# First two tiles of the second layer's attention projected two steps earlier, in a two-layer transformer block

## The reference

```python
def _layer(x, wqkv, qs, ksc, wo, lg, lb, w1, b1, w2, b2):
    h = shift_token(x)                       # second half of the features from the token before
    q, k, v = split(h @ wqkv)                # 8 heads of 64
    q, k = l2norm(q) * qs, l2norm(k) * ksc
    q, k = rotary_xpos(q, k)
    x = x + local_attention(q, k, v) @ wo
    h = shift_token(x)
    mu, var = h.mean(-1), h.var(-1)
    h = (h - mu) / sqrt(var + 1e-05) * lg + lb
    a, g = split(h @ w1 + b1)
    return x + (a * gelu(g)) @ w2 + b2

for l in range(2):                           # DEPTH
    x = _layer(x, wqkv[l], ...)
```

## Time and profile before

| | us |
|---|---|
| median of 3 runs | 1131.87 (1130.56 to 1132.34) |
| profiled execution, its own time | 1133.57 |
| profiled execution, span from first to last instruction | 1131.8 |
| TensorE busy in the span | 1062.1 |
| GpSimd busy in the span | 747.3 |
| VectorE busy in the span | 833.3 |
| ScalarE busy in the span | 670.9 |

### The profile page before, as it was taken

One profiled execution on the slowest core, in us unless ns is written; L12 is line 12 of the kernel. 1 busy time (PEld: TensorE's weight loads), 2 busy tenths in 40 slices (PEclk: granted clock), 3 DMA queues, 4 the chain that ended last, 5 costly groups with the idle time before them and its releaser, 6 DMA issues. The chain is left out here.

```text
span 1131.8 us, 23099 instructions
## 1 busy us (share of the span) xinstructions
PE 1062.1 (94%) x8304; PEld 654.9 (58%) x8304; DVE 833.3 (74%) x1522; ACT 670.9 (59%) x1222; POOL 747.3 (66%) x510
## 2 busy tenths in 40 slices
PE   6884799999999999999999999889999797999988
PEld 3552455555555555555555554766677694776778
DVE  6995666666666666666666674589999689999857
ACT  2552366566665665666666655047887556887744
POOL 3662466767686767776676768679986238756526
PEclk9996799999999999999999999999999999999989
DMA  8899622524315124242152100101111100111101
GB/s 255 276 275 357 161 57 48 112 53 93 80 50 122 40 66 104 67 92 69 48 113 71 44 20 21 38 10 32 33 43 34 25 2 19 33 34 33 44 17 36
DMA packets 82624, 88.48 MB, mean 78 GB/s; under 512 B 32036, under 2 KB 65360, under 8 KB 82512
## 3 DMA queue, kind: packets, MB, share of 16 engines
q1 hardware_dynamic: 82512, 87.01, 29.9%
HBM read 53.04 MB, written 24.24 MB: 68 GB/s over the span
## 5 line engine op out<-in xcount | busy, mean ns | idle before, releaser
L871 DVE CUSTOM_DVE_ANT_0 junk<-psum,alibi 128x1024 bf16<-128x1024 f32 x256 | 313.2, 1223 | 200.7 <-PE psum L942 191.8
L843 ACT ACTIVATE E<-psum,keybias_sb 128x1024 f32<-128x1024 f32 x256 | 274.7, 1112 | 229.6 <-PE psum L966 216.3
L774 POOL TENSOR_TENSOR sum_p<-sum_p,E 128x1024 f32<-128x1024 f32 x96 | 232.4, 2421 | 90.4 <-ACT E L843 85.8
L978 PE MATMUL psum<-E,V 128*64 128x512 f32 x1024 | 248.1, 605 | 0.0
L942 PE MATMUL psum<-KH,QH 64*128 64x512 f32 x512 | 118.7, 459 | 12.9 <-PEq L274 7.4
L978 PEld LDWEIGHTS psum<-E,V 128*64 128x64 f32 x1024 | 62.2, 136 | 112.3 <-issue 98.4
L780 POOL TENSOR_TENSOR sum_p<-sum_p,xpos_sb 128x1024 f32<-128x1024 f32 x32 | 76.3, 2384 | 69.0 <-DVE xpos_sb L881 69.0
L942 PEld LDWEIGHTS psum<-KH,QH 64*128 64x128 f32 x512 | 49.5, 189 | 121.9 <-DVE M L871 84.5
L966 PE MATMUL psum<-QH,KH 64*128 64x512 f32 x512 | 102.2, 395 | 2.1 <-DVE M L871 2.1
L966 PE MATMUL psum<-QL,KH 64*128 64x512 f32 x512 | 101.6, 392 | 0.0
L966 PE MATMUL psum<-QH,KL 64*128 64x512 f32 x512 | 101.5, 392 | 0.0
(11 more groups left out here) (149 smaller groups left out, 2008.3 us busy)
## 6 DMA issues: line engine op xcount, KB each, us to landing
QH<-qa_scratch SPq DMA_DIRECT2D x64, 256.0 KB, 4.2
qa_scratch<-tH SPq DMA_DIRECT2D x8, 1024.0 KB, 5.4
qa_scratch<-tL SPq DMA_DIRECT2D x8, 1024.0 KB, 7.9
QL<-qa_scratch SPq DMA_DIRECT2D x64, 128.0 KB, 4.2
vp_att<-v_att SPq DMA_DIRECT2D x64, 128.0 KB, 2.3
XF<-inverse_scratch SPq DMA_DIRECT2D x30, 256.0 KB, 3.4
KH<-k_scratch SPq DMA_DIRECT2D x16, 256.0 KB, 3.9
KL<-k_scratch SPq DMA_DIRECT2D x16, 256.0 KB, 5.1
```

What stands on the lines that cost most here:

```text
L774: pool.tensor_tensor(sum_p[:, s, :], first, E[:, k % 4, :], ALU.add)\
L843: act.activation(E[:, k % 4, :], scores(k % 2), ACT.Exp, bias=kb).then_inc(exp_done, 1)
L871: dve.tensor_tensor_reduce(junk[:, :], banks(max_bank(i, k), 2), alibi[:, s, :], -1.0, BIG, ALU.add, ALU.min, M[:, s, k:k + 1]).then_inc(m ...
L978: last = pe.matmul(banks(6 + i % 2)[HD * ch:HD * ch + HD, :], V[:, g, k, :], E[:, k % 4, ch * 512:(ch + 1) * 512], start=(k == 0), stop=(k ...
```

## The change

The stages of attention 1 with lags 0, 1 and 2 (TURN_X, PROJECT and NORMS, on all engines) run two steps earlier for tiles 0 and 1. They now stand in steps 31 to 34, where the MLP of layer 0 still works on its last tiles; for the other 14 tiles they keep their steps, and all stages with a lag of 3 and more are as before. Within a step the order of the stages is the same: each stage's early half stands where the stage stood.

```diff
-        parts = []
+        parts, second_attention = [], []
+        EARLY_TILES, EARLY_STEPS, EARLY_LAGS = 2, 2, 3
@@
+            if l > 0:
+                second_attention.append(attention)
             parts += [(attention, LAYER_STEPS * l)] + (output if l == 0 else []) + [(mlp, LAYER_STEPS * l + MLP_STEP)]
 
+        def early(fn, lag):
+
+            def some_tiles(t, s):
+                if t < EARLY_TILES:
+                    fn(t, s)
+
+            return some_tiles, lag - EARLY_STEPS
+
+        def other(fn, lag):
+
+            def some_tiles(t, s):
+                if t >= EARLY_TILES:
+                    fn(t, s)
+
+            return some_tiles, lag
+
         def stages(engine, handle):
 
-            return [(fn, lag + first) for part, first in parts if engine in part for fn, lag in part[engine](handle)]
+            found = []
+            for part, first in parts:
+                for fn, lag in part[engine](handle) if engine in part else ():
+                    if first >= LAYER_STEPS and lag < EARLY_LAGS and part in second_attention:
+                        found += [early(fn, lag + first), other(fn, lag + first)]
+                    else:
+                        found.append((fn, lag + first))
+            return found
```

## The result

The changed kernel took 1136.85 us (median of 11 runs, 1134.04 to 1138.42), the kernel before 1132.01 us beside it. The ratio is 1.0038, with a 95% interval of 1.0026 to 1.0051: slower by some 4.3 us, and by more than the 0.2% that can be told from no change. The forecast was 1135.3 us, +3.4, with a range of 1131.0 to 1137.0; inside it, the case of the forecast itself was given +2.8 to +4.2. The span went from 1131.8 to 1135.0 us. The lines of this kernel.py are 26 higher than before from the second half on (L1485 is the old L1459).

What follows compares the result with a forecast made beforehand. Latency where the two layers meet was taken to bound the kernel, not throughput. Terms 0.2 + 1.5 + 0.9 + 1.3 - 0.5 gave +3.4 us, median 1131.87 to 1135.3 us; range 1131.0 to 1137.0.

Steps and rivals of the forecast that it cites:

- the case of the forecast itself: Between the two layers, two delays of ln_apply by GpSimd's rotation plus a low TensorE clock: +2.8 to +4.2 us, chance 0.4.
- the seam: Stretch between the two layers, said to be latency-bound; measured from MLP tile 10's XF write to layer 1 tile 2's mask product.
- the power rival: GpSimd's power on tile 1 also blocks VectorE's normalise of tile 0 in layer 1: +4.5 us, 1136.4 us, chance 0.12.
- Term 1: Layer 1's first tiles: two long TensorE waits come back as three shorter ones, behind MLP turn, square and gate: +0.2 us.
- the ring: Pace-setting loop from project_qk through rotary products and square to the next project_qk; 5.25 us, 6.7 through ln_apply.
- Term 2: ln_apply of MLP tile 14 waits on VectorE for GpSimd's rotation additions of tile 0, delaying the second project_qk: +1.5 us.
- Term 3: TensorE falls to 1.2 GHz on layer 1's second project_qk, 3.20 instead of 1.88 us: +0.9 us.
- Term 4: ln_apply of MLP tile 15 waits on VectorE for GpSimd's two rotation additions of tile 1: +1.3 us.
- Term 5: VectorE's normalise of tile 1 in layer 1 takes some 1.4 instead of 1.96 us, with less GpSimd addition left: -0.5 us.
- The power: GpSimd's power of tile 1 overlaps VectorE's normalise of tile 0; no wait was taken, with a bound of +1.1 us.
- The faster rival: TensorE's 1.25 and 2.09 us waits between the layers really go: -3.3 us, or -4.6 without the low clock; chance 0.08.

## Why the prediction was right

The mechanism was right, and the seam's +3.58 us is close to the sum of +3.4. The whole time fits less well than that: the median of 1136.85 us lies only 0.15 below the top of the range, and the +4.3 us of the ratio is just outside the +2.8 to +4.2 of the forecast's own case and nearer to the +4.5 of the power rival. Only the rows tell these two apart. That the median still fell inside the range is partly luck.

By its own steps; positions in the changed trace are lowered by 0.46 us, by which TensorE's rows ahead of the seam lie later than in the earlier trace rows.

- *Term 1, the ring without collisions, +0.2.* With rotation and ln_apply parted, the first mask product came 20.23 us after the XF write of tile 10 (946.65 and 926.42) against 20.12 before: +0.1. The ring of 6.7 us is 6.65. Right in size; it came back as four waits, not three, and the +0.1 is taken against a kernel with a low clock.
- *Term 2, first collision, +1.5.* ln_apply ended at 931.70, forecast 931.8. Right, and the choice between its bounds too: the second addition goes ahead of ln_apply's second instruction in both traces.
- *Term 3, the clock, +0.9.* project_qk took 3.45 and 3.60 us; its last product ended at 938.36, forecast 938.2. The filled gaps, at 1.39 us, priced it together with what it does to the second collision.
- *Term 4, second collision, +1.3.* ln_apply of tile 15 ended at 941.03, forecast 940.8. Right in size, for a partly different reason: the rotation of tile 1 was released by the late products (0.42 us idle, DVE t_att, before 938.97), not by the end of the power.
- *Term 5, normalise of tile 1, -0.5.* 1.36 us instead of 1.96: -0.6.
- *Sum.* The first mask product stands at 949.45, forecast 949.2, and the seam is +3.58 (second traces: +3.71) where the sum said +3.4. By the experiments it is -0.47 without the collisions, where terms 1 and 5 said -0.3, and +4.05 for collisions and clock, where terms 2 to 4 said +3.7. The median's +4.3 has the seam's value in its interval. Its excess of 0.7 us over the seam is less than the part behind the last mask product varies from one execution to the next.
- *The power.* normalise of tile 0 ran from 946.80 to 948.02 with GpSimd's power from 944.98 to 947.91 around its start and took 1.22 us. It waited for nothing, as the prediction had it, in every trace of a kernel with the two tiles early (1.21 or 1.22 us). The prediction had argued from an ln_apply row, which has one tile as its input and not two, so that row alone could not decide it. The rule of the Trainium skill (SBUF — State Buffer, "Who interferes with whom"), by which the two exclude each other for the whole instruction, agrees with the rows of GpSimd's additions (normalise at 939.85) and not with that of its power. The rival with +4.5 us falls by this row.
- *The faster rival* named its own point of decision, VectorE at ln_apply before the rotation starts. It came 0.6 us after it (930.20 and 929.64). Even without the collisions the seam gained only 0.47 us, not 3.3, and that was the low clock: the waits came back behind ln_apply, turn and hT copy. With ln_apply out of the ring 1.9 us of them were gained (33.37 against 35.26 us), which shows that it was in the way; 1.51, 0.67 and 0.76 us of waits were still left on TensorE.

## What to carry to other kernels

Moving a stage ahead in an in-order schedule moves it behind other neighbours on every engine: write down, for each engine, what stands between a producer and its consumer in the new order before counting on an idle gap. When two stages that take turns between engines are interleaved, look first at the place of the one whose result feeds the longest chain. Here ln_apply of two tiles, four instructions of 128x64, moved by one step took 6.4 us from the changed kernel's seam (39.97 to 33.52), while the change itself had added 3.6; the whole time shows some 4 us of it (a ratio to the kernel before of 0.9999 instead of 1.0038). And look whether VectorE and GpSimd meet in the new order where they didn't before, since a short VectorE instruction can wait for a long GpSimd one. At last, when the whole time disagrees with the stretch that was changed, compare the traces outside it before looking for a cause in it.

## What was not expected of the hardware

- GpSimd's instructions differ in what they hold up on VectorE. Its 128x512 additions of 1.25 us delayed each ln_apply instruction that met one to their end plus 0.05 or 0.06 us, in all traces; its power on 128x16, 2.93 us long, delayed an instruction with two SBUF inputs by nothing that shows (1.22 us in all).
- The slow stretch of TensorE's clock stood behind a gap: filling the first gaps with idle transposes brought the work behind them back to 2.4 GHz (1.98 instead of 3.45 us), and a slow stretch then stood behind the next unfilled one.
- Behind the last mask product the same kernel ran at 2.4 GHz in one execution and partly at 1.2 GHz in another, with the same work in front of it; this makes 3.5 us of its time (56.4 and 59.9 us). In the seam the clock fell in the same place in both traces of each of the two kernels.
